# A graph network kernel: GpSimd's gathers 14 to 16 without their waits for the V products

## The chip, the cores and the metric

The kernel runs on one core of a Trainium2 chip. The metric is device time in microseconds (us), of one launch of the whole program, the median of three runs.

## What is computed

Two graph layers on 6250 nodes with 128 features and 200000 edges, which are sorted by destination. The first is an attention layer with 4 heads, the second sums neighbours and edge attributes and runs a small network. Cut to what matters:

```python
h  = relu(layernorm(x)); xp = h @ W                         # 6250 x 128
e  = leaky_relu(a_s[src] + a_d[dst])                        # one logit a head and edge
m  = segment_max(e, dst); e = exp(e - m[dst])
out = segment_sum(e / denom[dst] * xp[src], dst)            # 4 heads of 32
x  = x + relu(out + bias)
h  = relu(layernorm(x))
agg = segment_sum(edge_attr @ We + be, dst)
xc = concat(h, agg); neigh = segment_sum(xc[src], dst)
x  = x + relu((xc + neigh) @ W1 + b1) @ W2 + b2
```

## The kernel before

After a short start (normalising, projecting, a table of node rows in HBM) the edges are worked off in 87 groups of 128 x 18 edges. A last stage (49 matrix windows, TensorE) follows. The change lies in the loop over the groups.

For a group n, each engine has a body `item(n, b, it)` whose order is written out by hand; semaphores link the engines. b is n mod 2 and names the buffer.

- **GpSimd** (`gather`, L806 to L819, and `yield_to_chain`, L788 to L804) fills V[b]: 18 indirect DMAs, one for each column j of 128 edges, fetch a row of 144 floats (576 bytes) for each of 128 edges from the table. Gather j goes to `V[b][:, j, :]`. Before gathers 0, 6 and 12 it waits until the matching third of the group two before, which had the same buffer, has been multiplied (L812). While these gathers of group n+1 are issued, the other engines work on group n, and `yield_to_chain` makes GpSimd wait for them: before gather 6 for the tail matmul (`cback_b`), before 8 for the peak sums (`mg_b`), before 11 for the look-up (`look`), and before 14, 15 and 16 for one third each of the V products (`vm_b`).
- **VectorE** waits for all 18 gathers of group n and copies the logits out (L1638). Then scans, peaks and shifts follow in a long line of short operations (L1643 to L1717); behind the look-up sums come five short operations and, in thirds of 6 columns, the multiplication of V by the weights (L1742). Then come the "edge marks", six comparisons in bf16 (L1477, `tabb<-iotah,...`), for the adjacency of this group and the next; then two tiny operations of the next group and its wait for the gathers.
- **TensorE** runs in order the transposes and the tail matmul (L1138, L1142, L1144), part of the adjacency (L1123, L1125), peak sums (L1161), attribute sums (L1133), the look-up (L1177), more adjacency and attribute sums, then the V products in thirds (L1194; each third raises `vm_b`), and adjacency again.
- **ScalarE** (L852 is its helper) copies adjacency blocks out of PSUM, makes the fp32 selection matrix, and takes the exponentials. The first step of the next group is a copy `thruT<-pm`, behind all adjacency copies of this one.
- **SyncE** issues the plain DMAs in one order: among them the load of edge attributes of group n+2 (1152 KB, L453, when the attribute sums of n are through) and last the store of the adjacency of group n-1 (1568 KB, L526).

`vm_b` counts three for each group, so with n for the group being gathered `n * QN + (q + 1 - QN)` asks for q+1 thirds of group n-1, the one that the others work on. QN is 3, QUART 6, J 18.

Of the kernel before, what the change touches and what calls it, by code (L numbers as in the profile page):

```python
# [54 lines left out]
QN = 3  # L55
# [26 lines left out]
def gnn_kernel(nc, x, src, dst, attr, W, att_src, att_dst, bias0, We, be, W1, b1, W2, b2, out):  # L82
    ctx = ExitStack()
    with ctx:
# [3 lines left out]
        def sem(name):  # L88
            return ctx.enter_context(nc.semaphore(name))
# [210 lines left out]
        def s(name):  # L300
            if name not in S:
                S[name] = sem(name)
            return S[name]
# [390 lines left out]
        def _(pool):  # L694
# [93 lines left out]
            def yield_to_chain(n, j):  # L788

                if isinstance(n, int) and n == 0:  # L790
                    return
                if j == 6:
                    pool.wait_ge(s("cback_b"), n)
                    pool.sem_inc(s("g_started"), 1)
                if j == 8:
                    pool.wait_ge(s("mg_b"), n)
                    pool.sem_inc(s("g_started"), 1)
                if j == 11:
                    pool.wait_ge(s("look"), n)
                    pool.sem_inc(s("g_started"), 1)  # L800
                for q, at in enumerate((14, 15, 16)):
                    if j == at:
                        pool.wait_ge(s("vm_b"), n * QN + (q + 1 - QN))
                        pool.sem_inc(s("g_started"), 1)  # L804

            def gather(b, it, rows, table, index, gat, ix, n=None, chain=False):  # L806
                pool.wait_ge(s(f"{ix}{b}"), it * 16 + 16)
                pool.sem_inc(s("g_started"), 1)
                for j in range(J):
                    if n is not None and j % QUART == 0 and not (isinstance(n, int) and n < 2):  # L810

                        pool.wait_ge(s("vm_b"), n * QN + (j // QUART + 1 - 2 * QN))  # L812
                        pool.sem_inc(s("g_started"), 1)
                    if chain:
                        yield_to_chain(n, j)
                    pool.indirect_dma_start(  # L816
                        out=V[b][:, j, 0:rows], out_offset=None, in_=table,
                        in_offset=bass.IndirectOffsetOnAxis(ap=index[b][:, j:j + 1], axis=0))\
                        .then_inc(s(f"{gat}{b}"), 16)  # L819
# [1073 lines left out]
```

## Time and profile before

| what | value |
|---|---|
| median of 3 runs | 3118.07 us (3117.33 to 3122.89) |
| the profiled execution, its own time | 3102.13 us |
| its span in the profile | 3100.2 us |
| busy, of the span | PE 66%, VectorE 58%, GpSimd 54%, ScalarE 35% |
| DMA | 560.29 MB, 181 GB/s over the span |

The profiled execution lies 16 us (0.5%) below the median. The span is 2 us shorter than its own time. The busy shares are means over a short start, the loop over the groups, and the last stage, in which TensorE runs alone. A row of a timeline gives the start in us from the span's start, the length, engine, line, operation, out<-in; in brackets stands the idle time of the engine before it and what ended it.

### The profile page before, as it was taken

To read this page: it belongs to the slowest core of one execution; us is meant where nothing else is said; L and a number is where in the kernel's file an instruction comes from. 1 tells how busy PE (TensorE), PEld (TensorE's weight loads), DVE (VectorE), ACT (ScalarE), POOL (GpSimd) and SP (SyncE) were. 2 spreads that over 40 slices of the span, in tenths; PEclk is the share of its full clock that TensorE was granted. 3 is DMA by queue.
4 is the path that set the end of the run, shared out by engine and by line. 5 is a ranking of instruction groups with operands and counts; after the bars stand their busy time and mean duration, and the time that the engine had idled before them with its cause. 6 is when DMAs were issued, how large, how long until landed. Compare 5 with 4: busy or idle time off the path is not lost.

```text
span 3100.2 us, 64216 instructions
## 1 busy us (share of the span) xinstructions
PE 2043.0 (66%) x16208; PEld 1674.9 (54%) x16208; DVE 1807.2 (58%) x6198; ACT 1085.6 (35%) x2295; POOL 1673.2 (54%) x1626
## 2 busy tenths in 40 slices
PE   4365665665665655665656656656656656699998
PEld 3354554554554544554545545545545544588887
DVE  7566676665666666666666766766766766411111
ACT  3134344344434443443443443443444443300000
POOL 4566666666666666666666666666666666000000
PEclk8677777776777767777767777777777777799999
DMA  9855655655655555655556556556556555666654
GB/s 192 134 163 177 194 168 174 195 159 180 193 155 187 177 169 189 189 160 185 162 176 194 157 184 194 168 173 194 156 185 194 156 185 176 225 213 214 225 212 146
DMA packets 276907, 560.29 MB, mean 181 GB/s; under 512 B 113395, under 2 KB 211139, under 8 KB 248081
## 3 DMA queue, kind: packets, MB, share of 16 engines
q1 hardware_dynamic: 226763, 444.37, 42.5%
q0 software_dynamic: 50112, 115.56, 16.5%
q8 instruction: 12, 0.20, 0.0%
q14 instruction: 20, 0.16, 0.0%
HBM read 382.53 MB, written 177.22 MB: 181 GB/s over the span
## 4 chain that ended last, share of the span: by engine, by line
PE 41%; issue 20%; DVE 15%; DMA 9%; another core or an unknown queue 5%; SPq 3%; ACT 2%; POOL 2%; ACTq 1%; DVEq 1%; POOLq 0%
PE pv L1133 10%; PE pv L1248 9%; DMA big<-table,idx 8%; PE pv L1194 7%; PE pt L1248 4%; PE pt L1123 3%; PE pm L1161 2%; POOL big L816 2%; ACT xsb L852 2%; PE pa L1123 1%; DVE peaks L1513 1%; DVE tabb L1477 1%; PE pa L1177 1%; ACTq L905 1%
## 5 line engine op out<-in xcount | busy, mean ns | idle before, releaser
L816 POOL DMA_INDIRECT big<-table,idx x1566 | 1639.8, 1047 | 929.9 <-issue 414.2
L852 ACT ACTIVATE xsb<-pt 128x343 f32 x1042 | 477.8, 459 | 1213.3 <-PE pt L1125 567.1
L1133 PE MATMUL pv<-big 128*128 128x128 f32 x3132 | 523.6, 336 | 5.7 <-ACT big L852 3.5
L1133 PEld LDWEIGHTS pv<-big 128*128 128x128 f32 x3132 | 490.3, 246 | 36.1 <-issue 11.7
L1123 PE MATMUL pt<-tabb 128*128 128x343 bf16 x1042 | 400.0, 384 | 65.8 <-ACT xsb L852 36.5
L1194 PE MATMUL pv<-big 128*128 128x133 f32 x3132 | 391.3, 280 | 7.0 <-DVE big L1742 4.2
L1638 DVE COPY logit<-big 128x72 f32<-128x72 f32 x87 | 21.9, 252 | 608.6 <-DMA big<-table,idx 540.1
L1194 PEld LDWEIGHTS pv<-big 128*128 128x128 f32 x3132 | 367.8, 190 | 16.2 <-DVE big L1742 8.6
L1477 DVE TENSOR_TENSOR tabb<-iotah,keyp 128x2064 bf16<-128x2064 bf16 x261 | 319.7, 1225 | 0.0
L1142 PE MATMUL pm<-ident,pre 128*4 128x128 f32 x87 | 32.5, 374 | 433.9 <-DVE pre L1643 226.5
L1248 PE MATMUL pv<-big,xsb 128*128 128x384 bf16 (+1 forms) x1617 | 279.3, 330 | 18.5 <-DVE big L1779 18.5
L852 ACT ACTIVATE xsb<-pa 128x343 f32 x521 | 238.9, 458 | 95.0 <-ACT xsb L852 50.3
L1248 PEld LDWEIGHTS pv<-big,xsb 128*128 128x128 bf16 (+1 forms) x1617 | 230.4, 147 | 52.4 <-issue 21.4
L1142 PEld LDWEIGHTS pm<-ident,pre 128*4 128x4 f32 x87 | 7.2, 82 | 451.5 <-DVE pre L1643 236.4
L1742 DVE TENSOR_TENSOR big<-big,pm 128x768 f32<-128x768 f32 x261 | 233.4, 949 | 26.2 <-ACT pm L852 18.7
L1125 PE MATMUL pt<-tabb 128*128 128x49 bf16 x1041 | 224.9, 216 | 0.0
L1123 PE MATMUL pa<-tabb 128*128 128x343 bf16 x521 | 200.8, 385 | 28.3 <-issue 18.3
L1161 PE MATMUL pm<-peaks,selb 128*128 128x13 bf16 x1566 | 56.2, 174 | 228.8 <-DVE peaks L1513 143.7
L1123 PEld LDWEIGHTS pt<-tabb 128*128 128x128 bf16 x1042 | 114.9, 110 | 159.5 <-ACT xsb L852 63.1
L1161 PEld LDWEIGHTS pm<-peaks,selb 128*128 128x128 bf16 x1566 | 48.5, 105 | 261.2 <-DVE peaks L1513 157.2
L852 ACT ACTIVATE big<-selb 128x2304 f32<-128x2304 bf16 x87 | 184.1, 2116 | 1.0 <-DVE selb L1477 1.0
L852 ACT ACTIVATE fhT<-pt,b1s 128x128 f32<-128x128 f32 (+1 forms) x49 | 18.0, 367 | 388.6 <-PE pt L1225 388.6
(289 smaller groups left out, 2975.8 us busy)
## 6 DMA issues: line engine op xcount, KB each, us to landing
adj<-xsb SPq DMA_DIRECT2D x87, 1568.0 KB
big<-in_edge_attr_dram SPq DMA_DIRECT2D x87, 1152.0 KB
xsb<-adj SPq DMA_DIRECT2D x33, 1568.0 KB, 6.2
selb<-rel SPq DMA_DIRECT2D x87, 576.0 KB
tabb<-adj SPq DMA_DIRECT2D x16, 1568.0 KB, 6.2
big<-table,idx POOLq DMA_INDIRECT x1566
state<-sums SPq DMA_DIRECT2D x87, 130.5 KB
sums<-state SPq DMA_DIRECT2D x87, 130.5 KB
```

Source lines behind the costliest of these rows:

```text
L816: pool.indirect_dma_start(out=V[b][:, j, 0:rows], out_offset=None, in_=table, in_offset=bass.IndirectOffsetOnAxis(ap=index[b][:, j:j + 1], ...
L852: return nc.scalar.activation(out_, in_, func, **kw).then_inc(s(name), 1)
L905: _, at = nc.values_load_multi_w_load_instructions(offs[0:1, bass.DynSlice(n * OW + lo, hi - lo)], engines=[mybir.EngineType.Activation], ...
L1123: ins = nc.tensor.matmul(pab[c % 3], ohl[:, c, :], ohk[:, c, 0:KW], start=True, stop=alone)
L1125: ins = nc.tensor.matmul(pab[c % 3][:, 0:NB], ohl[:, (c - 1) % J, :], ohc[:, (c - 1) % J, 0:NB], start=False, stop=True)
L1133: ins = nc.tensor.matmul(sumA[b], SEL[b][:, j, :], AT[b][:, j, :], start=(j == 0), stop=(j == J - 1))
L1142: nc.tensor.transpose(tailT, pre1[:, :, J - 1], ident[:, :]).then_inc(s("tailT_b"), 1)
L1161: ins = nc.tensor.matmul(mg, selH[:, j, :], peaks[:, j, :], start=(j == 0), stop=(j == J - 1))
L1194: ins = nc.tensor.matmul(sumV[b], SEL[b][:, j, :], V[b][:, j, 0:TAB], start=(j == 0), stop=(j == J - 1))
L1248: ins = nc.tensor.matmul(pay[k][0:rows, 0:NK * C], adjT[k][:, 0:rows, h], yb[:, h, :], start=(h == 0), stop=(h == NB - 1))
L1477: return v.tensor_tensor(to.rearrange("p j (w e) -> p j w e", e=2), v_in, at, ALU.is_equal)
L1742: v.tensor_tensor(v4, v4, wps[:, js, :].rearrange("p j (h a) -> p j h a", a=1) .to_broadcast([128, QUART, H, F]), ALU.mult).then_inc(s("vw ...
```

## The change

The last loop of `yield_to_chain` is taken out: three waits on `vm_b`, ahead of gathers 14, 15 and 16, and with each an increment of the counter `g_started`, on which nothing waits.

```diff
                 if j == 11:
                     pool.wait_ge(s("look"), n)
                     pool.sem_inc(s("g_started"), 1)
-                for q, at in enumerate((14, 15, 16)):
-                    if j == at:
-                        pool.wait_ge(s("vm_b"), n * QN + (q + 1 - QN))
-                        pool.sem_inc(s("g_started"), 1)
```

## Rows read from the trace of the kernel before

**Rows 1.** The page: span, and the chain that ended last, by line.

```profile
span 3100.2 us, 64216 instructions
PE pv L1133 10%; PE pv L1248 9%; DMA big<-table,idx 8%; PE pv L1194 7%; PE pt L1248 4%; PE pt L1123 3%; PE pm L1161 2%; POOL big L816 2%; ACT xsb L852 2%; PE pa L1123 1%; DVE peaks L1513 1%; DVE tabb L1477 1%; PE pa L1177 1%; ACTq L905 1%
```

**Rows 2.** The logit copy: page's group (busy, mean, idle), then duration, first and last start.

```profile
L1638 DVE COPY logit<-big 128x72 f32<-128x72 f32 x87 | 21.9, 252 | 608.6 <-DMA big<-table,idx 540.1
L1638 DVE COPY logit<-big x87: 211/220/455, 126.2 to 2633.2; 128x72 f32<-128x72 f32 x87
```

**Rows 3.** Timeline of GpSimd: gathers 10, 13 to 17 of one group, 0 next.

```profile
1510.55 1.98 POOL L816 DMA_INDIRECT big<-table,idx  x1 [0.30 <-issue]
...
1515.36 0.94 POOL L816 DMA_INDIRECT big<-table,idx  x1 [0.30 <-issue]
1518.15 0.97 POOL L816 DMA_INDIRECT big<-table,idx  x1 [1.85 <-PE pv L1194]
1519.43 1.31 POOL L816 DMA_INDIRECT big<-table,idx  x1 [0.30 <-issue]
1521.77 0.94 POOL L816 DMA_INDIRECT big<-table,idx  x1 [1.04 <-PE pv L1194]
1523.02 0.94 POOL L816 DMA_INDIRECT big<-table,idx  x1 [0.30 <-issue]
1524.27 0.94 POOL L816 DMA_INDIRECT big<-table,idx  x1 [0.30 <-issue]
```

**Rows 4.** The chain in order of time: the gather's DMA, four groups in a row.

```profile
1493.46 3.83 DMA big<-table,idx
...
1523.02 5.15 DMA big<-table,idx
...
1552.02 5.06 DMA big<-table,idx
...
1582.15 3.85 DMA big<-table,idx
```

**Rows 5.** Waits of GpSimd over the span: us in total, times, longest.

```profile
POOL big L816 <- PE pv L1194: 192.3, 106, 3.7
```

**Rows 6.** Timeline of VectorE: V products, edge marks, first step of next group.

```profile
1510.48 1.23 DVE L1477 TENSOR_TENSOR tabb<-iotah,keyp 128x2064 bf16<-128x2064 bf16 x1
...
1513.79 2.68 DVE L1742 TENSOR_TENSOR big<-big,pm 128x768 f32<-128x768 f32 x3 [0.30 <-ACT pm L852]
...
1516.86 1.22 DVE L1477 TENSOR_TENSOR tabb<-iotah,keyp 128x2064 bf16<-128x2064 bf16 x1
...
1518.23 0.55 DVE L1477 TENSOR_TENSOR tabb<-iotah,lop 128x768 bf16<-128x768 bf16 x1
...
1518.70 1.22 DVE L1477 TENSOR_TENSOR tabb<-iotah,keyp 128x2064 bf16<-128x2064 bf16 x1
...
1520.14 0.18 DVE L1635 TENSOR_SCALAR cont<-isl 128x68 f32 x1
```

**Rows 7.** SyncE's queue, and busy time in 1522 to 1527 (clock, DMA share, GB/s last).

```profile
1517.23 0.33 SPq L453 DMA_DIRECT2D big<-in_edge_attr_dram  x1
...
1521.83 0.33 SPq L526 DMA_DIRECT2D adj<-xsb  x1
...
1522.00:1527.00 5.00, 1.17 (x7) 0.31 (x5) 0.00 (x0) 2.55 (x6) 3.78 (x5) 0.84 1.06 406
```

**Rows 8.** Timeline of the last group: its gather 17 and its logit copy.

```profile
2630.15 0.94 POOL L816 DMA_INDIRECT big<-table,idx  x1 [0.30 <-issue]
2633.18 0.22 DVE L1638 COPY logit<-big 128x72 f32<-128x72 f32 x1 [5.00 <-DMA big<-table,idx]
```

**Rows 9.** Other engines ahead of the logits: timeline, then the page's group.

```profile
1525.01 0.27 ACT L852 ACTIVATE thruT<-pm 4x128 f32<-4x128 f32 x1
...
1528.42 0.22 DVE L1638 COPY logit<-big 128x72 f32<-128x72 f32 x1 [8.10 <-DMA big<-table,idx]
...
L1142 PEld LDWEIGHTS pm<-ident,pre 128*4 128x4 f32 x87 | 7.2, 82 | 451.5 <-DVE pre L1643 236.4
```

**Rows 10.** VectorE's peaks, a group with a stall and the next without; the page's group.

```profile
1505.15 0.15 DVE L1585 TENSOR_SCALAR fy<-fve 128x1 int32<-128x1 int32 x1 [1.19 <-remote]
...
1506.61 0.56 PEld L1161 LDWEIGHTS pm<-peaks,selb 128*128 128x128 bf16 x18 [4.81 <-DVE peaks L1513]
...
1533.98 0.25 DVE L1513 TENSOR_TENSOR peaks<-pkr,peaks 128x72 bf16<-128x72 f32 x1
...
L1161 PEld LDWEIGHTS pm<-peaks,selb 128*128 128x128 bf16 x1566 | 48.5, 105 | 261.2 <-DVE peaks L1513 157.2
```

## The prediction, made before the changed kernel was run

> **What bounds the kernel.** I read the page first. Busy shares name TensorE, but the chain that ended last shows in its list of lines, beside TensorE's, 8% for the landing of gathers (`DMA big<-table,idx`) and 2% for GpSimd [rows 1]. The page's group for the logit copy says who is late: VectorE stood idle 608.6 us ahead of its 87 copies, 7.0 us a group, and the gathers' DMA ended nearly all of it [rows 2]. The first copy starts at 126.2 us and the last at 2633.2, so a group takes (2633.2 - 126.2) / 86 = 29.15 us [rows 2].
>
> Next, GpSimd's timeline in one group. Gathers follow each other every 1.25 us (0.94 and a gap of 0.30) unless they wait. Gather 13 is over at 1515.36 + 0.94 = 1516.30. Gather 14 starts at 1518.15 after an idle 1.85 that a V product ended, 15 follows at 1519.43, 16 at 1521.77 after 1.04, again ended by a V product, and 17 at 1523.02 [rows 3]. From there the chain goes over the gather's DMA, 5.15 us, to the logit copy at 1528.42 [rows 4, 9]. So the loop now closes over: logits, line of short operations, look-up, attribute sums, V products, gathers 16 and 17, landing, logits of the next group. The three waits lie on it.
>
> **Part 1, the waits go.** Over the span GpSimd waited 192.3 us for V products, in 106 gaps [rows 5]. A gather that waits for nothing has a gap of 0.30 before it all the same [rows 3], so 192.3 - 106 x 0.30 = 160 us are the waits' own, 1.86 for each of the 86 groups whose gathers have them (group 0's do not). In the group shown it is 1.55 + 0.74 = 2.29 us. Other waits of GpSimd are tied to tail, peak sums and look-up, which are steps of the same group and stay at their distance from the logits; they neither grow nor shrink. The increments of `g_started` stood in the shadow of the waits; I count them at nothing, their cover being the gap of 0.30 that stays.
>
> **Part 2, gathers 14 to 17 move under the edge marks.** With no wait, 14 starts at 1516.60 in the group shown, 15 to 17 at 1.25 each, the last at 1520.35. That is the stretch in which VectorE makes its edge marks, from behind the V products (1513.79 + 2.68) to 1520.14 [rows 6]. Gathers are stretched by the long mark (`keyp`, 1.22 us): the one at 1510.55, which starts just behind such a mark's start (1510.48), takes 1.98 us instead of 0.94, that is 1.03 more; the one at 1519.43, which meets one (1518.70) late, takes 1.31, or 0.37 more; the one at 1518.15, mostly beside the short mark at 1518.23, takes 0.97 [rows 3, 6]. Two long marks lie in the new path of 14 and 15, and each gather meets its mark with a part only. I take 0.35 for each, by the row of partial overlap, 0.70 in all, less the 0.40 that 14 and 15 pay already in the rows: 0.3 us a group, 26 us. The bounds are nothing (a loss of this kind below zero would be the 0.40 paid now that falls away, 34 us of gain) and twice 1.03 less 0.40, 1.66 us a group, 143 us.
>
> The Trainium skill bears on this ("SBUF — State Buffer", section "Who interferes with whom"). It says that a VectorE instruction with two SBUF inputs contends with a GpSimd instruction that reads SBUF, and, of the shared ports, that whoever comes first keeps them and the other is blocked fully. The edge marks have two SBUF inputs and a gather reads its indices. Taken strictly, that would hold GpSimd through the whole train of marks. The rows agree for the long mark only in part: 1.03 us and 0.37 us, and almost nothing beside the short one. What it would do here is the first rival below.
>
> **Part 3, the landing.** From the issue of gather 17 to the chain's next step the DMA took 3.83, 5.15, 5.06 and 3.85 us in four groups, 4.47 in the mean [rows 4]. In this stretch the attribute load (issued 1517.23) and the adjacency store (1521.83) fill the DMA engines: 406 GB/s and a DMA share of 1.06 in 1522 to 1527 [rows 7]. In the last group the logit copy starts 3.03 us behind gather 17 [rows 8]; less the 0.25 between the end of landing and the copy (1523.02 + 5.15 to 1528.42) this is 2.8, the nearest row of an easier landing. The new gather 17 starts before the adjacency store is issued, but still amid the attribute load. So relief of up to 4.47 - 2.8 = 1.7 us a group is possible (146 us); so is a worse landing, since four gathers now come close together: up to 5.15 - 4.47 = 0.7 a group (60 us). I take no change, as both kinds of neighbour were there before too.
>
> **What is late next.** TensorE's transpose of the first scan stood idle 451.5 us, 5.2 a group, and ended its waiting with the scan behind the logits [rows 9]. ScalarE's `thruT` copy ends at 1525.28, 3.1 us ahead of the logit copy at 1528.42 [rows 9]; what needs it comes behind the first scan. VectorE is free from 1520.3. All three have more than the 1.56 us that I count on. The reuse of V[b] waits for the first third of the group two before; gather 0 of the next group now starts at 1524.27 and would start near 1522.3 (1520.35 + 0.70 + 1.25), while the first third was done at 1518.15 [rows 3]. It stays covered. Gather 17 to gather 8 of the next group is held by the logits as before.
>
> **The sum.** 160 - 26 + 0 = 134 us, 1.56 us a group, off the profiled execution: 3102 - 134 = 2968 us. The median stands 16 us above the profiled execution, and I carry this over: 3118 - 134 = **2984 us**. With the bounds of part 2 (+143 in place of +26, or -34) and part 3 (-146, +60) the forecast's own range is about 2900 to 3060.
>
> **Rivals.**
> - *The marks hold the gathers.* If GpSimd is blocked to the end of the marks near 1520.15, gather 14 ends there, 15 starts at 1520.5, 16 at 1521.75, 17 at 1523.0: where it starts now (1523.02). No gain, 3118 us. For it: the 1.98 row. Against: 0.97 beside the short mark and 1.31 beside the long one. Chance 0.08. The skill's rule strictly read (full block) is this case.
> - *The landing gets easier.* Gather 17 escapes the adjacency store in many groups. At half the bound, 0.85 us a group, it gives 73 us more: 2911 us; at the full bound 2838, where ScalarE's 3.1 us and TensorE's 5.2 begin to count. For it: 3.83 and 3.85 beside 5.15. Against: the attribute load is in the way. Chance 0.17.
> - *Slower: the stall in the peaks comes into every group.* In some groups VectorE's split of the peaks stalls (1.19 us idle at 1505.15, "remote", more behind it), and TensorE idles 4.81 us ahead of the peak sums; in the next group the same line runs through by 1533.98. The mean idle is 261.2 / 87 = 3.0 us [rows 10]. The cause is not in the rows. If it has to do with DMA traffic behind the logits, it may grow, because the adjacency store now reaches past the logit copy. In every group it costs 4.81 - 3.0 = 1.8 us, 155 us: 3118 - 134 + 155 = 3139 us. It decides from 1.56 us a group on. Against: all of today's chain before the gathers keeps its own phase. Chance 0.14.
> - *The landing is paced by the store.* If gathers get through only as the adjacency store ends, 17's earlier issue is worth nothing; the store's time hangs on the chain and stays. 3118 us. Against: landings differ by 1.3 us from group to group, which a fixed pace by the store does not give at once [rows 4]. Chance 0.03.
> - *The change does nothing.* It would need that the waits were met already; rows 5 exclude that. No chance counted.
>
> **Chances and range.** Forecast 0.58, easier landing 0.17, slower 0.14, marks 0.08, store 0.03. A measurement of this kernel tells about 0.2% (6 us) from no change. Faster: 0.58 + 0.17 = 0.75; same: 0.08 + 0.03 = 0.11; slower 0.14. To hold 8 in 10, the range goes from 2880 (leaving a part of the easier landing out, some 0.05) to 3124 (leaving the slower case out).
>
> **What would show it.** Right: no gap of GpSimd ended by a V product before gathers 14 to 16; gather 17 about 1.5 us nearer to gather 8; VectorE's idle before the logit copy near 7.0 - 1.56 = 5.4 us; a group near 27.6 us. Part 2 is wrong if gathers 14 and 15 take near 2 us each; part 3 if the DMA behind gather 17 leaves 4.5 us by more than half a microsecond; the slower rival holds if TensorE's idle before the peak sums goes from 3.0 toward 4.8 us. The prediction fails as a whole if another engine, above all ScalarE at `thruT`, is what the next logits' line waits for.

## The result, and the profile after

The changed kernel takes 3068.3 us in the median (3065.5 to 3071.2), the kernel before 3117.7 (3109.6 to 3122.9) beside it: a ratio of 0.985, 95% interval 0.9825 to 0.9868. It is faster by 49 us. The forecast was 134 us: right in sign, inside the range, and too large by a factor of nearly three.

The profiled execution fell from 3102.1 to 3065.5 us, by 36.6 only: the one profiled before lies 16 us below its median, this one 3 us. The account below is of these two executions. The page of the changed kernel, its groups of instructions; lines lie four lower than before (L1638 is L1634, L816 is L812, L1194 is L1190, L852 is L848, L1142 is L1138):

```profile
span 3063.6 us, 63790 instructions
...
L812 POOL DMA_INDIRECT big<-table,idx x1566 | 1683.8, 1075 | 847.3 <-issue 398.8
...
L1190 PE MATMUL pv<-big 128*128 128x133 f32 x3132 | 482.2, 293 | 120.1 <-issue 118.1
...
L1634 DVE COPY logit<-big 128x72 f32<-128x72 f32 x87 | 21.1, 242 | 311.3 <-DMA big<-table,idx 277.1
```

The durations, first and last start of the logit copy:

```profile
L1634 DVE COPY logit<-big x87: 210/221/449, 133.1 to 2594.0; 128x72 f32<-128x72 f32 x87
```

VectorE's idle ahead of it fell from 608.6 [rows 2] to 311.3 us, by 3.4 us a group, but a group takes (2594.0 - 133.1) / 86 = 28.62 us instead of 29.15: only 0.53 shorter. The other 2.9 us of waiting went elsewhere. TensorE's V products (L1190), which had stood idle 7.0 us in all, stand 120.1. The account closes: 86 x 0.53 = 46 us gained in the loop, 6.9 us lost ahead of the first logits (133.1 against 126.2, where the removed waits do not act; the kernel before with narrow copies, h2 below, has 129.5 on another chip, so a part may be difference between executions), 2.6 us in the last stage (469.6 behind the last logits against 467.0); 36.6 us in the span.

Where it went, the waits of the changed kernel tell (us in total, times, longest):

```profile
DVE logit L1634 <- DMA big<-table,idx: 277.1, 77, 7.3
...
POOL big L812 <- remote: 276.8, 175, 2.6
...
DVE pen L1685 <- remote: 118.3, 64, 2.4
...
PE pm L1138 <- ACT thruT L848: 112.0, 72, 1.7
...
DVE tails L1647 <- PE pm L1138: 105.3, 57, 3.2
```

No wait of GpSimd for a V product stands ahead of gathers 14 to 16. Two waits are new: the scan behind the logits (`tails`) waits for TensorE's transposes, and these for ScalarE's copy `thruT`. In the kernel before, `tails` had stood 2.6 us in all, and TensorE's transpose had waited 0.5 us for `thruT`. A third new wait, ahead of gather 0, is shown below.

The table holds means over groups 3 to 84, worked out from the starts of the records, in us behind the logit copy of the same group n (in both kernels, the profiled executions).

| step | before | after | difference |
|---|---|---|---|
| `tails` scan starts | 2.15 | 3.72 | +1.57 |
| peak sums' last record ends (TensorE) | 7.61 | 8.51 | +0.90 |
| `pen`, which needs them, starts (VectorE) | 8.54 | 10.53 | +1.99 |
| gather 8 of group n+1 | 9.24 | 11.29 | +2.05 |
| V products start | 17.11 | 20.23 | +3.12 |
| their last third ends | 21.89 | 27.66 | +5.77 |
| gather 17 of n+1 | 24.36 | 24.78 | +0.42 |
| `thruT` copy of n+1 ends | 26.39 | 31.85 | +5.46 |
| logit copy of n+1 | 29.19 | 28.69 | -0.50 |

From gather 8 to gather 17 the way fell from 15.12 to 13.49, a gain of 1.63 us. From 17 to the logits it fell from 4.83 to 3.91, a gain of 0.92. From the logits to gather 8 it grew by 2.05. The net is 0.50.

The loss of 2.05 has three parts: `tails` starts 1.57 later, the way from `tails` to the last peak sum is 0.67 shorter, and the way from there to `pen` is 1.09 longer.

One group of the changed kernel shows where TensorE gets late. Timeline of TensorE and, in the last two rows, of ScalarE and VectorE:

```profile
1524.58 2.97 PE L1190 MATMUL pv<-big 128*128 128x133 f32 x24
...
1527.82 0.39 PE L1190 MATMUL pv<-big 128*128 128x133 f32 x2
1528.44 0.40 PE L1190 MATMUL pv<-big 128*128 128x133 f32 x2 [0.22 <-issue]
1529.21 0.35 PE L1190 MATMUL pv<-big 128*128 128x133 f32 x1 [0.38 <-issue]
1530.64 1.04 PE L1190 MATMUL pv<-big 128*128 128x133 f32 x7 [1.08 <-issue]
...
1533.92 0.27 PE L1134 MATMUL pm<-ident,thru 128*4 128x128 f32 x1
...
1535.46 0.25 ACT L848 ACTIVATE thruT<-pm 4x128 f32<-4x128 f32 x1
...
1532.14 0.36 DVE L1634 COPY logit<-big 128x72 f32<-128x72 f32 x1 [2.95 <-DMA big<-table,idx]
1536.22 0.41 DVE L1647 TENSOR_TENSOR_SCAN tails<-thruT,pm 4x128 f32<-4x128 f32 x1 [1.78 <-PE pm L1138]
```

By their records 24 V products run through in 2.97 us; the last 12 take from 1527.82 to 1531.68, 3.9 us, with gaps that no semaphore ends ("issue"). Adjacency follows on TensorE and ScalarE, and `thruT` comes at 1535.46, 3.3 us behind the logits; in the kernel before it stood 3.4 us ahead of them (1525.01 against 1528.42 [rows 9]).

The ends of matmul records are modelled. The trace also holds the times at which semaphores rose, and they tell more: `vm_b` rose for the first third at 1530.76, though the last product of that third has its record at 1525.91 to 1526.18, and for the second at 1530.89 (record's end 1527.54). In the mean over the 53 groups in which all three increments were recorded, the first two came 4.57 and 3.30 us behind the records' ends; in the kernel before it was 0.26 and 0.01 (80 groups), and 0.01 and 0.01 in e4, on a faster chip. So TensorE's results are late from the first third on, and not only in the last. Gather 0 of the next group but one, which needs the first third for its buffer, now waits for it (GpSimd, gathers 17 and 0):

```profile
1528.77 1.06 POOL L812 DMA_INDIRECT big<-table,idx  x1 [0.30 <-issue]
1531.54 0.94 POOL L812 DMA_INDIRECT big<-table,idx  x1 [1.70 <-remote]
```

GpSimd is idle 1.44 us ahead of gather 0 in the mean, where it was 0.30. This is off the chain: ahead of gather 8 it still stands 2.11 us.

### The profile page after: what moved, and what is told of

Its sections match the earlier page's. It is cut to its first block, busy times and chain, and to the rows that moved or that the text cites. A ratio compares the mean times of both kernels' runs of the same rounds, so it can differ in the third digit from the quotient of the medians.

```text
span 3063.6 us, 63790 instructions
## 1 busy us (share of the span) xinstructions
PE 2197.7 (72%) x16208; PEld 1748.5 (57%) x16208; DVE 1823.4 (60%) x6198; ACT 1074.7 (35%) x2295; POOL 1717.1 (56%) x1626
## 4 chain that ended last, share of the span: by engine, by line
PE 37%; issue 22%; DVE 10%; another core or an unknown queue 7%; POOL 7%; ACT 7%; ACTq 4%; DMA 4%; SPq 3%; DVEq 1%; POOLq 0%
PE pv L1244 9%; PE pv L1129 9%; POOL big L812 7%; PE pv L1190 6%; ACT xsb L848 5%; PE pt L1244 4%; ACTq L901 3%; DMA big<-table,idx 3%; PE pt L1119 2%; PE pa L1173 2%; ACT big L848 1%; PE pa L1119 1%; PE pt L1121 1%; PE pm L1157 1%
## 5 line engine op out<-in xcount | busy, mean ns | idle before, releaser
L812 POOL DMA_INDIRECT big<-table,idx x1566 | 1683.8, 1075 | 847.3 <-issue 398.8
L848 ACT ACTIVATE xsb<-pt 128x343 f32 x1042 | 477.5, 458 | 963.1 <-remote 371.9
L1129 PE MATMUL pv<-big 128*128 128x128 f32 x3132 | 549.7, 348 | 78.7 <-ACT big L848 47.6
L1129 PEld LDWEIGHTS pv<-big 128*128 128x128 f32 x3132 | 515.2, 257 | 120.3 <-issue 82.9
L1190 PE MATMUL pv<-big 128*128 128x133 f32 x3132 | 482.2, 293 | 120.1 <-issue 118.1
L1190 PEld LDWEIGHTS pv<-big 128*128 128x128 f32 x3132 | 410.4, 196 | 176.8 <-issue 169.4
L1119 PE MATMUL pt<-tabb 128*128 128x343 bf16 x1042 | 418.9, 402 | 58.7 <-ACT xsb L848 36.6
L1473 DVE TENSOR_TENSOR tabb<-iotah,keyp 128x2064 bf16<-128x2064 bf16 x261 | 319.8, 1225 | 0.0
L848 ACT ACTIVATE xsb<-pa 128x343 f32 x521 | 238.9, 459 | 158.7 <-PE pt L1121 53.3
L1119 PE MATMUL pa<-tabb 128*128 128x343 bf16 x521 | 209.4, 402 | 53.7 <-ACT xsb L848 32.7
L1121 PE MATMUL pt<-tabb 128*128 128x49 bf16 x1041 | 232.4, 223 | 0.0
L1634 DVE COPY logit<-big 128x72 f32<-128x72 f32 x87 | 21.1, 242 | 311.3 <-DMA big<-table,idx 277.1
L1473 DVE TENSOR_TENSOR tabb<-iotah,lop 128x768 bf16<-128x768 bf16 x261 | 144.8, 555 | 69.0 <-remote 61.6
L848 ACT ACTIVATE big<-selb 128x2304 f32<-128x2304 bf16 x87 | 184.1, 2116 | 1.0 <-DVE selb L1473 1.0
L1157 PEld LDWEIGHTS pm<-peaks,selb 128*128 128x128 bf16 x1566 | 48.5, 105 | 210.2 <-DVE peaks L1509 98.1
L848 ACT ACTIVATE fhT<-pt,b1s 128x128 f32<-128x128 f32 (+1 forms) x49 | 18.0, 367 | 388.5 <-PE pt L1221 388.5
L848 ACT ACTIVATE fhT<-pa 128x256 f32<-128x256 f32 x87 | 33.4, 384 | 339.0 <-remote 249.9
```

The source lines that it names most:

```text
L812: pool.indirect_dma_start(out=V[b][:, j, 0:rows], out_offset=None, in_=table, in_offset=bass.IndirectOffsetOnAxis(ap=index[b][:, j:j + 1], ...
L848: return nc.scalar.activation(out_, in_, func, **kw).then_inc(s(name), 1)
L1119: ins = nc.tensor.matmul(pab[c % 3], ohl[:, c, :], ohk[:, c, 0:KW], start=True, stop=alone)
L1121: ins = nc.tensor.matmul(pab[c % 3][:, 0:NB], ohl[:, (c - 1) % J, :], ohc[:, (c - 1) % J, 0:NB], start=False, stop=True)
L1129: ins = nc.tensor.matmul(sumA[b], SEL[b][:, j, :], AT[b][:, j, :], start=(j == 0), stop=(j == J - 1))
L1157: ins = nc.tensor.matmul(mg, selH[:, j, :], peaks[:, j, :], start=(j == 0), stop=(j == J - 1))
```

## The experiments

The same kernel is not equally fast on all chips. Two sets of runs fell on chips on which the kernel before takes 2849 us ("faster"), three on chips on which it takes 3111 to 3183 ("slower"), as where the result was taken (3118). Each set names the time of the kernel before beside it. "A", "C", "D" and so on in the expectations are the theories of that moment.

**Which of the waits counts (faster chip, 2848.8 us).** One wait alone is kept, in the kernel before: the one ahead of gather 14 (e1, below) or, with `((2, 16),)` in its place, the one ahead of 16 (e2).

```diff
-                for q, at in enumerate((14, 15, 16)):
+                for q, at in ((0, 14),):
```

> Only the wait ahead of gather 14 stays (first third of the V products); those ahead of 15 and 16 are gone. Theory A (the gather side lost its weight: with earlier logits the order of TensorE and ScalarE, adjacency copies and then the thruT copy, closes the loop): this wait is nearly all of the idle time (1.55 of 1.86 us a group), so the loop stays mostly bound by gathers and this kernel lies within 0.3% of before, 3105 to 3120 us. Theory B (gathers that run beside the last third of the V products slow TensorE there, which eats the gain): gather 17 still runs later than the last third starts, a part of the slowing shows, and the time lies between before and after, nearer to after, 3070 to 3095 us.

> Only the wait ahead of gather 16 stays (last third); 14 and 15 go free. Theory A: gather 16 starts some 0.5 us earlier than before, since 15 is through, and the loop is bound by gathers again: about 3118 - 45 = 3073 us, close to after, with the last third of the V products at its length of before. Theory B: no gather 16 or 17 runs beside the last third, so the slowing is gone while half a microsecond is gained: as fast as or faster than after, 3050 to 3075 us, and TensorE's idle time inside the V products back from 120 us to under 20. What tells A from B here is that idle time, more than the total.

Measured: 2850.5 us with the first wait (1.0005, 0.9988 to 1.0022), 2832.2 with the last (0.9946, 0.9930 to 0.9962). The theories had expected e1 between 3070 and 3120 us and e2 between 3050 and 3075, times of a slower chip. On this chip the wait ahead of 14 is the whole price of the three. That price isn't the moment of gather 17, which is issued 21.84 us behind the logits in e1 and 21.67 in e2. What differs is gathers 14 and 15, which e2 issues 1.49 and 1.78 us earlier; its next logits come 0.29 us earlier (25.91 against 26.20).

**Narrow adjacency copies, same batch.** ScalarE's copies of the adjacency take 49 of 343 columns, in the kernel before (e3) and in the changed one (e4). If ScalarE's `thruT` bounds the changed kernel, e4 must gain and e3 not.

```diff
-   a(adjE[b][:, bass.DynSlice(at[c - lo], KW)], pab[c % 3], ACT.Copy, "ab_ev")
+   a(adjE[b][:, bass.DynSlice(at[c - lo], 49)], pab[c % 3][:, 0:49], ACT.Copy, "ab_ev")
```

> Before, with the adjacency copies of ScalarE cut from 343 to 49 columns each (a part of the adjacency is left out). Theory A: in before these copies hide under the wait for gathers; shorter copies change nothing but ScalarE's busy time: 3100 to 3118 us, within 0.5% of before. Theory B expects the same. It is the base for the next kernel.

> After, with the adjacency copies cut from 343 to 49 columns (a part of the adjacency is left out). Theory A: the order of ScalarE and TensorE was what took back the gain; some 4 us less of copies a group frees it, and the full gain of part 1 and 2 of the prediction comes out: 2970 to 3000 us, 70 us or more below after. Theory B: the slowing of TensorE in the last third stays and is not ScalarE's, so the time stays within 25 us of after, 3045 to 3070 us.

Measured: 2828.8 us (0.9933, 0.9915 to 0.9952) and 2828.6 (0.9923, 0.9900 to 0.9947): with narrow copies the three waits are worth nothing, and the gain that theory A called for does not come. The changed kernel with full copies wasn't run here. The chain in order of time, the DMA of the last gather, first in three groups of e3, then of e4:

```profile
1496.83 3.97 DMA big<-table,idx
...
1522.54 4.44 DMA big<-table,idx
...
1549.34 4.12 DMA big<-table,idx
```

```profile
1500.58 5.34 DMA big<-table,idx
...
1526.22 5.76 DMA big<-table,idx
...
1552.27 5.60 DMA big<-table,idx
```

Gather 17 is issued 1.40 us earlier in e4 (20.31 us behind the logits against 21.71, means over the groups) and its landing takes that much longer; the period is 25.99 against 25.96 us. In both, the store's last packet ends shortly ahead of the logits: at 24.95 and 25.33, with the last increment of the gathers' semaphore at 25.94 and 25.97. From group to group the logits move with the store's end (correlation 0.98 in e3, 0.85 in e4; 1 would be a fixed bond, 0 none) and not, in e4, with the issue of gather 17 (0.03). This fits the rival "paced by the store", which had been given 0.03. No run on this chip moved the store, so here it is argued; f1 below moves it on another.

**The store as the cause (slower chip, 3169.5 us).** The changed kernel again (e5); the adjacency store issued near the start of SyncE's round, in the kernel before (f1) and the changed one (f2); and half the store, 64 of 128 partitions, and half its load in the last stage (f3). f1 and f2 also have three increments of a counter of SyncE, left out below.

```diff
                     store_sums(n - 1, base_before)
+                    store_adjacency(n - 1, 1 - b)
                 store_peak(n, b, base)
...
-                if not before_first:
-                    store_adjacency(n - 1, 1 - b)
```

```diff
-   sp.dma_start(adj[:, bass.DynSlice(head, 128), :].rearrange(...), adjE[b])
+   sp.dma_start(adj[0:64, bass.DynSlice(head, 128), :].rearrange(...), adjE[b][0:64, :])
```

> The changed kernel as it is, to have it on the same chip as the kernels beside it. The runs so far came from a chip on which the kernel before takes 2849 us, not 3118. Theory C (gather 17's data land only as the adjacency store of 1568 KB ends, whatever the time of its issue; in the kernels with full and narrow copies the landing came within 0.4 us of the store's end): within 0.8% below before, as the store's issue hangs on the chain. Theory A (TensorE's and ScalarE's order closes the loop): the same here; this run is the base.

> Before (all waits), with the adjacency store of the group before issued on SyncE ahead of the peak store, some 13 us earlier in the group, where the DMA engines are at 0.2 to 0.5 of their time. Theory C: gather 17 lands after about 2.6 us, not 4.3, so 1 to 1.7 us a group go: 3 to 5% faster than before. Theory A: gathers' landing is not the limit, under 1% change.

> The changed kernel with the same early store. Theory C: with the store out of the way the removal of the waits gives its 1.4 us a group on top: 1.3 to 1.6 us a group faster than the kernel before with the early store, so 8 to 10% below before in all, if TensorE and ScalarE allow it (their thruT copy ends 2.3 us ahead of the logits, so they will take a part: 6 to 8%). Theory A: no faster than the changed kernel as it is.

> The changed kernel with the adjacency store cut to 64 of 128 partitions, 784 KB instead of 1568 (the other half of the adjacency is left out, in the store and in the last stage's load). Theory C: the store ends about 2.6 us earlier and gather 17 lands up to that much earlier: 3 to 6% below the changed kernel. Theory A: within 1% of the changed kernel, but for the last stage, whose loads are halved (it is bound by TensorE, so under 10 us).

Measured against the kernel before: e5 0.9824 (0.9784 to 0.9863), f1 1.0047 (1.0024 to 1.0071), f2 0.9865 (0.9825 to 0.9904), f3 0.9848 (0.9808 to 0.9887). Neither another place nor half the size of the store gives the changed kernel anything here: on the slower chips the store is not its limit. f2 and f3 miss what theory C expected of them (8 to 10% and 3 to 6%), and f1, which it had 3 to 5% faster, is 0.5% slower. But f1 confirms one half of the theory, the landing. Means over groups 3 to 84, us behind the logits (g3, explained further down, has the attribute load late):

| kernel, chip | gather 17 issued | next logits | between | store's last packet | attribute load's last packet |
|---|---|---|---|---|---|
| before, slower | 24.36 | 29.19 | 4.83 | 28.38 | 22.80 |
| f1, slower | 27.46 | 30.09 | 2.63 | 14.59 | 26.37 |
| changed, slower | 24.78 | 28.69 | 3.91 | 33.30 | 26.75 |
| f2, slower | 25.01 | 29.42 | 4.40 | 15.98 | 29.09 |
| g3, slower | 26.44 | 29.20 | 2.75 | 35.84 | behind the logits |
| e3, faster | 21.71 | 25.96 | 4.25 | 24.95 | 19.69 |
| e4, faster | 20.31 | 25.99 | 5.68 | 25.33 | 19.89 |

Where neither large transfer is in flight behind gather 17 (f1, g3), the way to the logits takes 2.63 and 2.75 us; beside the store it takes 4.83, beside the attribute load 3.91 and 4.40. What f1 gains there it loses ahead: gather 8 comes at 11.65 instead of 9.24, and gather 14 waits for the V products as before. The changed kernel left the store behind and met the attribute load.

The groups of the V products, of f1, e5 and f3 (busy, mean of one, idle):

```profile
L1196 PE MATMUL pv<-big 128*128 128x133 f32 x3132 | 391.0, 279 | 1.5 <-DVE big L1744 1.4
```

```profile
L1190 PE MATMUL pv<-big 128*128 128x133 f32 x3132 | 481.4, 300 | 138.9 <-issue 134.4
```

```profile
L1190 PE MATMUL pv<-big 128*128 128x133 f32 x3132 | 499.1, 303 | 166.9 <-issue 160.7 <-DVE big L1738 4.4
```

With the waits the V products run without gaps (1.5 us over the span), without them TensorE stands 139 to 167 us, wherever the store lies (f2: 163).

**What makes the V products stand (slower chip, 3182.8 us).** The changed kernel again (g1); the last wait alone (g2) and the first alone (g4), the edits of e2 and e1; and the changed kernel with the attribute load behind the V products (g3). If gathers 16 and 17 beside the last third do it, g2 must cure it; if the attribute load does, g3 must.

```diff
-                if ahead is not None:
-                    load_attributes(n + 2, b, ahead)
...
                     store_adjacency(n - 1, 1 - b)
+                if ahead is not None:
+                    sp.wait_ge(s("vm_b"), n * QN + QN)
+                    sp.sem_inc(s("sp_turn"), 1)
+                    load_attributes(n + 2, b, ahead)
```

> The changed kernel once more, as base on this chip. On a chip where the kernel before takes about 3120 to 3170 us: 1.5 to 1.8% below before, with TensorE idle 120 to 140 us inside the V products (7 us before). On a chip where before takes about 2850 us: 0.3 to 0.8% below, with under 20 us of such idle time.

> Only the wait ahead of gather 16 stays. Theory D (on the slower kind of chip TensorE gets its matmuls of the last third one by one, 0.7 us apart, while gathers 16 and 17 are issued beside it, about 2.4 us a group, and ScalarE's and TensorE's order then closes the loop): with 16 and 17 held back the idle time inside the V products falls from 120 to 140 us to under 30 us, and the time is as good as after's or better, 1.5 to 3% below before. Rival E (the idle time has to do with the moment of the last third against other transfers, not with gathers beside it): the idle time stays over 60 us and the kernel lies between before and after.

> The changed kernel with the attribute load (1152 KB) issued last in SyncE's group, behind the adjacency store and a wait for all three thirds of the V products, so that it isn't in flight beside the last third. Rival E: TensorE's idle time inside the V products falls under 40 us and the kernel gains 1 to 3% on after. Theory D: the idle time stays over 90 us and the time within 1% of after. On the faster kind of chip gather 17 would land up to 1.3 us earlier, 1 to 4% below after, if the landing and not TensorE is what counts.

> Only the wait ahead of gather 14 stays. Theory D: gathers 15 to 17 run beside the last third as in after, less the time that 14 held them; idle time inside the V products over 60 us, 0 to 1.2% below before. Rival E: much the same; on the faster kind of chip within 0.2% of before, as in the first run.

Measured: g1 0.9802 (0.9768 to 0.9837), g2 1.0160 (1.0120 to 1.0199), g3 0.9760 (0.9726 to 0.9794), g4 1.0152 (1.0108 to 1.0196). The V products of g2, g3 and g4:

```profile
L1194 PE MATMUL pv<-big 128*128 128x133 f32 x3132 | 439.1, 284 | 108.6 <-issue 91.6 <-DVE big L1742 11.3
```

```profile
L1192 PE MATMUL pv<-big 128*128 128x133 f32 x3132 | 495.7, 301 | 170.0 <-issue 165.2 <-DVE big L1740 3.1
```

```profile
L1194 PE MATMUL pv<-big 128*128 128x133 f32 x3132 | 395.0, 280 | 11.5 <-issue 7.4 <-DVE big L1742 3.4
```

Neither is the cause: TensorE stands 108.6 us with gathers 16 and 17 held back, and 170.0 us with the load out of the way, as in g1 (169.6). And the effect is not monotone: either wait alone makes the kernel 1.5% slower here than all three do, and having none makes it 2% faster. No expectation had this. In g2 the increment for the last third comes at 23.64 us behind the logits (22.10 in the kernel before, on the result's chip), and gather 16, which waits for it, stands 3.63 us. On the faster chip the last wait alone had been a gain of 0.5%. g3 is the fastest version here (3108.2 us, 3105.6 to 3116.1, against g1's 3117.6 to 3124.1) and beats both kernels.

**The narrow copies again (slower chip, 3111.4 us).** The question of e3 and e4 on a chip on which the V products stand: h1 is e4's kernel, h2 e3's, h3 the changed kernel, h4 is g3 with narrow copies.

> The changed kernel whose adjacency copies take 49 of 343 columns; the other columns of the adjacency are left out. Theory A (the adjacency stage on TensorE and ScalarE sets the tails in the changed kernel): the copies are over some 2 us or more earlier, the wait of the tails for the order vanishes, and it runs 1 to 2 us per group under h3, 0.95 to 0.97 of the kernel before. Rival (the landing with the store sets the period): as h3 within 0.5 per cent, and the distance from the issue of gather 17 to the logits grows by what was gained. If this chip shows no steps of 0.70 us, both expect what the first batch showed, 0.992 of the kernel before.

> The kernel before with the same narrow adjacency copies (the same part of the adjacency left out). Theory A: the order was ready ahead of the logits already, so it gains at most 0.7 per cent, as on the first chip: 0.990 to 1.000 of the kernel before. Rival: the same as h1 within 0.3 per cent.

> The changed kernel itself, as the base of this batch. On a chip with the steps: 0.980 to 0.985 of the kernel before. On a chip without them theory A expects more than that, 0.96 to 0.98, since the stage on TensorE is not stretched; the rival expects about 0.99, what the narrow kernels gave there.

> The changed kernel with the attribute load issued last and the narrow adjacency copies (same part left out): whether anything but the landing is left. Theory A: within 0.5 per cent of h1. Rival: the load no longer competes with the last gathers, so their landing is 0.5 to 1 us shorter and it runs 1 to 3 per cent under h1.

Measured: h1 0.9819 (0.9801 to 0.9837), h2 0.9988 (0.9968 to 1.0008), h3 0.9850 (0.9832 to 0.9868), h4 0.9815 (0.9797 to 0.9832). The narrow copies bring the changed kernel 0.3%, 9 us, where theory A had expected 0.95 to 0.97 of the kernel before, at least 48 us under h3. They did act: the wait of `tails` for the transposes fell from 116.2 us in h3 to 84.3 in h1, and it starts 3.16 us behind the logits instead of 3.80. But the group did not get shorter: 28.64 us against 28.62. The gain went into the next wait, `pen` for the peak sums, 100.2 in h3 and 224.7 in h1:

```profile
DVE pen L1685 <- remote: 100.2, 53, 3.0
```

```profile
DVE pen L1685 <- remote: 224.7, 71, 4.2
```

In h4 this wait stands in nearly every group (85 of 87). Its timeline (TensorE, VectorE, ScalarE, GpSimd), then the busy time in three stretches of 1 us (PE, PEld, VectorE, ScalarE, GpSimd, then clock, DMA share, GB/s):

```profile
1561.53 0.65 PE L1159 MATMUL pm<-peaks,selb 128*128 128x13 bf16 x18 [2.32 <-DVE peaks L1505]
...
1562.63 0.25 PE L1123 MATMUL pa<-tabb 128*128 128x49 bf16 x1
1565.20 0.47 PE L1121 MATMUL pt<-tabb 128*128 128x343 bf16 x1 [2.32 <-ACT xsb L850]
...
1562.38 0.22 DVE L1594 SCALAR_TENSOR_TENSOR fy<-fy,fve 128x1 f32<-128x1 f32 x1
1565.11 0.16 DVE L1687 TENSOR_SCALAR pen<-pm 128x1 f32<-128x1 f32 x1 [2.51 <-remote]
...
1564.93 0.21 ACT L850 ACTIVATE xsb<-pt 128x49 f32 x1 [2.62 <-remote]
...
1562.69 0.94 POOL L814 DMA_INDIRECT big<-table,idx  x1 [0.30 <-issue]
1565.86 0.95 POOL L814 DMA_INDIRECT big<-table,idx  x1 [2.23 <-remote]
```

```profile
1562.00:1563.00 1.00, 0.88 (x11) 0.28 (x8) 0.60 (x3) 0.21 (x1) 0.69 (x2) 0.50 1.01 415
1563.00:1564.00 1.00, 0.00 (x0) 0.00 (x0) 0.00 (x0) 0.00 (x0) 0.63 (x1) 0.50 1.03 374
1564.00:1565.00 1.00, 0.00 (x0) 0.00 (x0) 0.00 (x0) 0.07 (x1) 0.00 (x0) 0.50 0.53 69
```

By its record the last peak sum was over at 1562.18, but what needs it starts at 1565.11 on VectorE and at 1565.86 on GpSimd, and TensorE and ScalarE stand too. For two microseconds no compute engine starts anything. All of them are waiting for TensorE: the semaphore of the peak sums rises at 1565.09, 2.9 us behind the record, and the one that ScalarE's copy needs at 1564.82. In this group the stretch ends as the transfers run out (374, then 69 GB/s); whether one has to do with the other is not shown. From the last record to the increment it is 0.86 us in the mean in the kernel before, 2.01 in the changed one, 3.17 in h1, 3.77 in h4 and 3.28 in f1; it is 0.01 in every kernel profiled on a faster chip. The stall of [rows 10] is another one, ahead of the peak sums.

**A break in the run of gathers (faster chip, 2849.7 us).** In the traces of the slower chips the slow stretches lie late in unbroken runs of gathers, and each removed wait was a break in such a run. Four memsets of GpSimd make a break that needs no V product, ahead of gather 15 (i1) or of gather 3 (i2), in the changed kernel.

```diff
+                        if j == 15 and not (isinstance(n, int) and n == 0):
+                            ...
+                            for q in range(4):
+                                pool.memset(wcat[32 * q:32 * q + 32, :], 0.0).then_inc(s("paused"), 1)
```

> The changed kernel with four short memsets of GpSimd (an estimate of 0.2 us each by the trace's memsets of that size, some 1 us with their gaps) ahead of gather 15, so the run 11 to 17 is broken without a wait for V products. Theory G: TensorE's idle ahead of the V products falls from 120 to 170 us to under 60, as in the kernel before; the time stays at 0.975 to 0.990 of the kernel before, though 15 to 17 are some 1 us later. Rival (the break does nothing for the other engines): that idle stays over 100 us, and the gathers' delay of 1 us a group comes in full or in part: 0.99 to 1.015.

> The changed kernel with the same four memsets ahead of gather 3 of the next group, in the run 0 to 7, which then ends near the peak sums. Theory G: the stretch from the end of the peak sums to their successor on VectorE shrinks from 2.0 us toward 0.9, gather 8 comes 0.5 to 1.1 us nearer to the logits, and it runs at 0.95 to 0.98 of the kernel before, faster than the changed kernel. Rival: gathers 3 to 7 are 1 us later, and either nothing changes (0.983 to 0.988) or gather 8 is later by part of it (to 1.01).

Measured: i1 1.0004 (0.9983 to 1.0024), i2 0.9950 (0.9932 to 0.9968). The V products of i1, on this chip:

```profile
L1196 PE MATMUL pv<-big 128*128 128x133 f32 x3132 | 390.7, 279 | 0.0
```

They have no gap here with or without the break (0.0 in e1 to e4 too), so the theory was not put to the test and stays open; the 0.95 to 0.98 expected of i2 was meant for a slower chip. What i2 does show: its break costs the last gathers nothing (17 is issued at 20.29 us, as in e4), and without the waits and with full copies the gain on such a chip is 0.5%. The store's last packet ends at 25.23 us and the logits follow at 25.99, as in e4; their correlation is 0.98, and -0.04 with gather 17. In i1 gather 15 comes 0.86 us later than in i2 and gather 17 1.24 us later, and the gain is gone; since e2 keeps it with gather 17 at 21.67, the issue of gather 17 alone can't be the reason. The changed kernel itself was not run on a faster chip.

## Why the prediction was right or wrong

**The chain that bounds the kernel before** was read rightly as far as GpSimd: the three waits lay on it, and gather 17 came nearer to gather 8 without them. That the landing behind it was paced by the store, the table with f1 shows.

**Parts 1 and 2** came out. Together they were to bring gather 17 nearer to gather 8 by 1.56 us; it was 1.63. The marks stretch gathers 14 to 16 by 0.84 us a group (4.59 us from the start of 14 to that of 17, less 3 x 1.25) where 0.70 was taken; but gathers 14 and 15 had paid 0.69 in the mean before (1.17 + 1.40 - 2 x 0.94), not the 0.40 of the group shown. So part 2 cost 0.15 us where 0.30 was taken, within its bounds. All gathers took 1075 ns in the mean instead of 1047, and the long mark `keyp` 1225 ns in both kernels: only GpSimd pays. The first rival falls: gathers are not held through the whole train of marks. But the full block itself, the exclusive lock of the Trainium skill ("SBUF — State Buffer", "Who interferes with whom"), is borne out for the one mark that runs as a gather starts. In the changed kernel 222 gathers start inside a long mark; 0.71 us of the mark are left in the mean, and the gather takes 0.59 more than 0.94, with a correlation of 1.00. The rows that the prediction read as partial overlap say the same: 0.49 us left of the mark and 0.37 more, 1.16 left and 1.03 more [rows 3, 6].

**Part 3, the landing**, was 0.92 us a group shorter where no change was taken, inside the bound of 1.7. The reason is the one the rival named, but by another way: the adjacency store needs all of ScalarE's adjacency copies, these became late with the V products, and so the store is now issued 28.2 us behind the logits instead of 22.8, and its first packet starts at 28.9, behind the landing. The attribute load, now ending at 26.75, kept the rest: f1 and g3 show 2.63 and 2.75 us with neither in flight, near the 2.8 of the bound. On the faster chip, where nothing becomes late, the store still ends just ahead of the logits.

**The range of the sum.** "About 2900 to 3060" is not what its bounds add up to: 3118 less (160 + 34 + 146) is 2778, less (160 - 143 - 60) is 3161. The measured 3068 lies outside the narrower range and inside the wider one; that it lies inside the stated 2880 to 3124 owes to the room left for the rivals.

**The step that failed** is the sentence that all other waits of GpSimd "stay at their distance from the logits", with the list of what is late next. Gather 8 moved 2.05 us away from them: 2.05 x 86 = 176 us, a term that the sum put at nothing, against 79 us more from the landing and 6 from parts 1 and 2. So 134 + 79 + 6 - 176 = 43 us are left. The landing's 79 us were luck and hid nearly half of the error. The cover was read from one group and for a single lap: ScalarE's `thruT` 3.1 us ahead of the logits. In the mean it was 2.8 us (29.19 - 26.39). From `tails` to the end of the next `thruT` TensorE and ScalarE now take 28.13 us instead of 24.24, 3.89 more. The last third of the V products takes 3.88 us instead of 1.53, which no term of the sum held; the way from the peak sums to `pen` grew by 1.09, and that from `pen` to the V products by 1.13; the rest shrank by 0.7 in sum. And `thruT` of the next group hangs on the logits of this one by way of TensorE, which works in order, so each lateness at `tails` comes back in the next lap: `tails` +1.57, V products +3.12, `thruT` +5.46 us. What the prediction put last, another engine at `thruT` holding the next logits' line, is what came. Its sentence that the reuse of V[b] "stays covered" failed too: the first third is reported 26.64 us behind the logits and gather 0 could start at 26.24. Gather 8's own wait swallows that.

**But `thruT` is not the bound by itself.** h1 started `tails` 0.6 us earlier and the peak sums gave it back. Three waits share the loop now: the landing (VectorE idle 277 us for it), the transposes (105) and the peak sums (118). The slower rival, a stall in the peaks, is there in part: the way from the peak sums to `pen` grew from 0.93 to 2.02 us, 1.1 of the 1.8 it was priced at. TensorE's idle ahead of them, the sign that was named for it, fell instead from 261.2 to 210.2 us: the stall moved behind them.

**Left open** is why TensorE reports its V products and peak sums so late on the slower chips. Both stalls go with increments that come late. So the 2.05 us are traced down to those increments, and no run took them away. Excluded as sole causes of the stall in the V products by runs: gathers 16 and 17 beside it (g2), the attribute load (g3), place and size of the adjacency store (f2, f3), ScalarE's long copies (h1). Unbroken runs of gathers are argued only. TensorE's granted clock is hardly a candidate between the two kernels (0.727 before and 0.732 after, in the loop), but it was not tested between the chips.

## What to carry to other kernels

A wait taken off the chain is worth no more than the smallest cover on the way round the loop, and the cover has to be read for the whole lap, including what the next iteration's first step needs from the slowest engine of this one. Read where the large transfers start and end against the landing one waits for: in e4 a gather issued 1.40 us earlier beside the same store landed no earlier. Where a profile shows an engine done and its waiters idle, look at the semaphore's own times. And time such a change on more than one chip: here the same edit (one wait left) gave 0.995 on one and 1.016 on another.

## What the runs showed of the hardware

- The kernel before took 2849 us on two chips, 3111 to 3183 on three others and 3118 where the result was taken, at a mean granted clock of 0.79 on the first two and 0.76 on the three. How much of the 9% the clock makes isn't shown.
- On the slower chips instructions that wait for nothing start 0.70 us apart, or 1.4, in stretches, on TensorE and SyncE at the same moments, as in the last third above (TensorE at 1528.44, 1529.21 and 1530.64, SyncE at 1529.16, 1529.88 and 1530.59). Added up over TensorE, SyncE and ScalarE, start to start, distances of 0.66 to 0.78 and 1.34 to 1.50 us make about 330 us in the kernel before, 670 in the changed one, 620 in h4, and 130 to 170 on the faster chips, where nearly all of it is ScalarE's. The Trainium skill ("Runtime: NRT & Kernel Launch", "Instruction fetch mechanics") calls the refill of an engine's instruction memory mostly hidden and names a stall behind a taken branch; the steps above lie inside a loop body, and no run here shows whether they are fetches.
- TensorE's semaphore increments can come late behind the records of its matmuls: 4.57 us for the first third of the V products and 2.01 for the peak sums in the changed kernel, 0.01 in every kernel profiled on a faster chip.
- The last gather's data come 2.63 and 2.75 us behind its issue with no large transfer in flight (f1, g3), 4.83 beside a store of 1568 KB, 3.91 and 4.40 beside a load of 1152 KB (times up to the logits).
- A gather of 0.94 us that starts inside a bf16 comparison of 1.22 us takes longer by what is left of it, less 0.12 us (222 gathers of the changed kernel); the comparison stays at 1.225 us.
- One wait of three left in place can be worse than all three (1.016 and 1.015 on the slower chip).
